# Gathering one turn's rows in a four-layer graph network: part of GpSimd's indirect gathers goes to SyncE as single-row copies

## What is computed

```
for layer in (gated, attention 4 heads, attention 8 heads + edge features + MLP, two GAT layers of 4 heads):
    per edge:  score from rows of the node tables at src[e] and dst[e]
    per edge:  weight = sigmoid(score)  or  softmax of the scores over the edges of one dst
    agg[node] = sum over the edges with dst == node of weight * row[src[e]]
    x = layernorm(x + dense(agg))
```

## Time and profile before

| | |
|---|---|
| runs, median of 3 | 7559.2 us (7523.48 to 7564.5) |
| profiled execution: its span | 6570.3 us, 37158 instructions recorded |
| profiled execution: its own time | not given |
| VectorE busy | 4654.6 us (71%) |
| GpSimd busy | 4293.2 us (65%) |
| ScalarE busy | 1375.2 us (21%) |
| TensorE busy | 1251.3 us (19%) |
| gathers in the four walks (L725) | 3136, 944 ns median |

### The profile page before, as it was taken

One profiled execution on the slowest core, in us unless ns is written; L12 is line 12 of the kernel. 1 busy time (PEld: TensorE's weight loads), 2 busy tenths in 40 slices (PEclk: granted clock), 3 DMA queues, 4 the chain that ended last, 5 costly groups with the idle time before them and its releaser, 6 DMA issues. The chain is left out here.

```text
span 6570.3 us, 37158 instructions
## 1 busy us (share of the span) xinstructions
PE 1251.3 (19%) x8049; PEld 1094.3 (17%) x8049; DVE 4654.6 (71%) x9455; ACT 1375.2 (21%) x3580; POOL 4293.2 (65%) x4445
## 2 busy tenths in 40 slices
PE   7100000145555534332000000810000010000000
PEld 6100000135544433322000000610000010000000
DVE  7788888799999969987888887744444444444445
ACT  0122222220111114431000000622222211222223
POOL 0777777667777760027777775367777767777775
PEclk9555555555555555556555555955555555555555
DMA  9666666433443437754666664123333323333332
GB/s 391 199 218 202 202 199 204 130 106 131 132 136 133 133 115 292 295 184 153 220 219 218 225 218 158 30 85 109 113 111 109 115 74 90 112 113 109 113 111 82
DMA packets 338944, 1032.97 MB, mean 157 GB/s; under 512 B 100325, under 2 KB 163137, under 8 KB 331294
## 3 DMA queue, kind: packets, MB, share of 16 engines
q0 software_dynamic: 166752, 401.68, 21.4%
q1 hardware_dynamic: 116642, 342.34, 14.8%
q10 hardware_dynamic: 55324, 286.57, 12.1%
HBM read 602.97 MB, written 427.39 MB: 157 GB/s over the span
## 5 line engine op out<-in xcount | busy, mean ns | idle before, releaser
L725 POOL DMA_INDIRECT rows<-table,idx x3136 | 2987.4, 953 | 985.0 <-issue 973.1
L644 POOL DMA_INDIRECT by_src<-ebuf,place x784 | 767.4, 979 | 275.0 <-issue 238.3
L1296 DVE SCALAR_TENSOR_TENSOR psA<-psA,cont,dstf 128x128 f32<-128x128 f32 (+1 forms) x2349 | 836.6, 356 | 48.0 <-ACT ebuf L1025 27.2
L1285 DVE TENSOR_TENSOR sc<-rows,ebuf 128x56 f32<-128x56 f32 x112 | 28.2, 252 | 1023.9 <-DMA rows<-table,idx 1023.9
L958 PE MATMUL psA<-dstf,ones 128*128 128x512 f32 x10 | 9.9, 1113 | 3055.3 <-DVE dstf L2223 3055.3
L1296 DVE SCALAR_TENSOR_TENSOR sums<-sums,cont,psA 128x128 f32<-128x128 f32 (+1 forms) x1512 | 518.9, 343 | 30.3 <-ACT psA L1221 29.0
L958 PEld LDWEIGHTS psA<-dstf,ones 128*128 128x128 f32 x10 | 2.7, 317 | 3056.9 <-issue 3056.9
L823 PE MATMUL psA<-attr,sums 128*128 128x49 f32 x1568 | 406.1, 403 | 470.8 <-DVE attr L1475 470.8
L2104 DVE TENSOR_TENSOR_SCAN psA<-rows,psA 128x1980 f32<-128x1980 f32 x112 | 480.0, 4286 | 3.9
L823 PEld LDWEIGHTS psA<-attr,sums 128*128 128x128 f32 x1568 | 397.0, 326 | 476.9 <-DVE attr L1475 476.9
L1227 ACT ACTIVATE psA<-df 128x60 f32<-128x60 f32 (+1 forms) x168 | 40.4, 241 | 1714.2 <-DVE df L1285 1714.2
(11 more groups left out here) (350 smaller groups left out, 5533.6 us busy)
## 6 DMA issues: line engine op xcount, KB each, us to landing
dstf<-spread_wide SPq DMA_DIRECT2D x168, 924.0 KB
states<-sums ACTq DMA_DIRECT2D x150, 952.0 KB, 4.0
rows<-by_src SPq DMA_DIRECT2D x55, 1035.0 KB, 5.1
states<-sums ACTq DMA_DIRECT2D x56, 1008.0 KB, 5.7
spread_wide<-sums SPq DMA_DIRECT2D x56, 924.0 KB, 24.7
states<-sums ACTq DMA_DIRECT2D x56, 903.0 KB, 7.4
rows<-table,idx POOLq DMA_INDIRECT x3136
msg<-low_rows SPq DMA_DIRECT2D x56, 448.0 KB, 3.7
```

The lines of the kernel that those rows point to most:

```text
L644: pool.indirect_dma_start(by_src[:, :], bass.IndirectOffsetOnAxis(ap=place[:, s, j:j + 1], axis=0), payload[:, s, j, :], None).then_inc(so ...
L725: pool.indirect_dma_start(rows[:, at:at + GW[ph]], None, table[ph][:, :], bass.IndirectOffsetOnAxis(ap=idx[:, s, j:j + 1], axis=0)).then_i ...
L1285: return dve.tensor_tensor(o_, a_, b_, op)
L1296: return dve.scalar_tensor_tensor(o_, a_, s_, b_, op0, op1)
```

## The change

Turn 54 (`SIDE`) of each walk no longer uses a half of `rows`. Its 14 columns go into a tile of its own (`ebuf`, `aux`, `msg`, `msg`). The first 10 (walks one and two) or 12 columns (three and four) are fetched by SyncE, partition by partition: one register load of 10 or 12 row numbers from `src`, then one single-row copy per number, whose HBM address comes from the register. That is 128 x 10 or 128 x 12 copies in a walk. GpSimd gathers the other 4 or 2 columns. The remaining 55 turns alternate between the two halves of `rows`, so turn 55 takes the half that turn 52 had.

In walks one and two SyncE's copies are divided over its iterations g = 1 to 52, each part behind the load L590 of that g and ahead of the load of the next; in walks three and four all stand in one piece behind L585.

GpSimd now takes the row numbers straight from `src`. The tile `idx`, ScalarE's copies into it and its semaphore are gone. In their place GpSimd waits once per walk for `src_in` and `n_kept`. `src` loses its 28 columns of padding, a one-hot tile of phase 0 moves from `ebuf` to `msg`, and one semaphore of the first-edge lookup is merged into another. VectorE waits at turn 54 for both `side_landed` and `side_gathered`.

```diff
+SIDE = 54
+SIDE_COLS = {0: 10, 2: 10, 3: 12, 4: 12}
...
-        src = sb("src", [P, CH + 2 * B], I32)
+        src = sb("src", [P, CH], I32)
...
-        hotSH = hot_turned(ebuf, 0, NB)
+        hotSH = hot_turned(msg, 1024, NB)
...
+        side_tile = {0: ebuf, 2: aux[:, :, :].rearrange("p b d -> p (b d)"), 3: msg, 4: msg}
...
+        def row_slot(ph, g):
+            return None if g == SIDE else (g - int(g > SIDE)) % 2
+        def slot_turns(ph, s, g=NG):
+            return sum(row_slot(ph, k) == s for k in range(g))
+        def landed_at(ph, g):
+            s = row_slot(ph, g)
+            before = sum(slot_turns(q, s) for q in TURN if q < ph)
+            return 16 * B * (before + slot_turns(ph, s, g) + 1)
+        def side_gathered_at(ph):
+            return 16 * sum(B - n for q, n in SIDE_COLS.items() if q <= ph)
+        def free_at(ph, g):
+            s = row_slot(ph, g)
+            users = [k for k in range(g) if row_slot(ph, k) == s]
+            return 2 + TURN[ph] * NG + (users[-1] + 1 if users else 0)
+        def turn_rows(ph, g):
+            s = row_slot(ph, g)
+            tile = side_tile[ph][:, 0:B * GW[ph]] if s is None else rows[:, s * B * GW[ph]:(s + 1) * B * GW[ph]]
+            return tile.rearrange("p (b w) -> p b w", b=B)
...
+            numbers_of = [sp.alloc_register(f"side_row{j}") for j in range(B)]
+            def side_open(ph):
+                sp.wait_ge(src_in, 48)
+                if ph == 0:
+                    sp.wait_ge(chains_ready, 1)
+                    sp.wait_ge(bias3_ready, 1)
+                    for k in range(2):
+                        sp.wait_ge(tab_first[k], 16 * -(-(KG - k) // 2))
+                else:
+                    sp.wait_ge(tab_saved, 16 * KG * TURN[ph])
+                    sp.wait_ge(n_kept, (2 if ph == 2 else 3) * KG)
+            def side_rows(ph, parts):
+                w, at, n = GW[ph], SIDE * B, SIDE_COLS[ph]
+                for p in parts:
+                    sp.load(numbers_of[0:n], src[p:p + 1, at:at + n])
+                    for j in range(n):
+                        node = sp.snap(numbers_of[j])
+                        sp.dma_start(side_tile[ph][p:p + 1, j * w:(j + 1) * w], table[ph][bass.ds(node, 1), :]).then_inc(side_landed[ph], 16)
...
                 if ZW[ph] == 4:
                     sp.dma_start(dflat[:, 0:CH * 4], view.rearrange("p c d -> p (c d)")).then_inc(slim_in, 16)
+                    side_open(ph)
+                    side_rows(ph, range(P))
 
...
                         if ph == 1 and g < NG - 1:
                             low_digits(g + 1)
+                        if ph in SIDE_COLS and g == 1:
+                            side_open(ph)
+                        if ph in SIDE_COLS and 1 <= g < SIDE - 1:
+                            side_rows(ph, range((g - 1) * P // (SIDE - 2), g * P // (SIDE - 2)))
                 if ph == 0:
...
-                    for it in range(IT):
-                        for s in range(2):
-                            g = it * 2 + s
-                            pool.wait_ge(idx_staged, g + (1 + TURN[ph] * (NG + 2)))
-                            pool.wait_ge(rows_used, g + (1 + TURN[ph] * NG))
-                            if g == 1 and ph < 3:
-                                spreads_landed()
-                            for j in range(B):
-                                at = (s * B + j) * GW[ph]
-                                pool.indirect_dma_start(rows[:, at:at + GW[ph]], None, table[ph][:, :],
-                                                        bass.IndirectOffsetOnAxis(ap=idx[:, s, j:j + 1], axis=0)).then_inc(rows_landed[s], 16)
+                    pool.wait_ge(src_in, 48)
+                    if ph:
+                        pool.wait_ge(n_kept, (2 if ph == 2 else 3) * KG)
+                    for g in range(NG):
+                        s = row_slot(ph, g)
+                        if s is None:
+                            for j in range(SIDE_COLS[ph], B):
+                                pool.indirect_dma_start(side_tile[ph][:, j * GW[ph]:(j + 1) * GW[ph]], None, table[ph][:, :],
+                                                        bass.IndirectOffsetOnAxis(ap=src[:, g * B + j:g * B + j + 1], axis=0)).then_inc(side_gathered, 16)
+                            continue
+                        pool.wait_ge(rows_used, free_at(ph, g))
+                        if g == 1 and ph < 3:
+                            spreads_landed()
+                        for j in range(B):
+                            at = (s * B + j) * GW[ph]
+                            pool.indirect_dma_start(rows[:, at:at + GW[ph]], None, table[ph][:, :],
+                                                    bass.IndirectOffsetOnAxis(ap=src[:, g * B + j:g * B + j + 1], axis=0)).then_inc(rows_landed[s], 16)
 
                     for s in range(2):
                         pool.wait_ge(sums_saved[s], 16 + 16 * IT * (TURN[ph] + 1))
...
-                else:
-                    act.wait_ge(rows_used, 2 + TURN[ph] * NG)
-                    for s in range(2):
-                        act.activation(idx[:, s, :], src[:, s * B:(s + 1) * B], ACT.Copy).then_inc(idx_staged, 1)
...
-                                at = (s * B + j) * GW[0] + D
-                                m = act.activation(gated[:, j * D:(j + 1) * D], rows[:, at:at + D], ACT.Copy, scale=wt[:, s, j:j + 1])
+                                m = act.activation(gated[:, j * D:(j + 1) * D], turn_rows(0, g)[:, j, D:2 * D], ACT.Copy, scale=wt[:, s, j:j + 1])
...
-                        act.wait_ge(rows_used, g + (3 + TURN[ph] * NG))
-                        act.activation(idx[:, s, :], src[:, bass.ds((g + 2) * B, B)], ACT.Copy).then_inc(idx_staged, 1)
...
-                        G3 = rows[:, s * B * GW[ph]:(s + 1) * B * GW[ph]].rearrange("p (b w) -> p b w", b=B)
+                        G3 = turn_rows(ph, g)
-                        dve.wait_ge(rows_landed[s], it * (16 * B) + (16 * B + TURN[ph] * IT * 16 * B))
+                        if row_slot(ph, g) is None:
+                            dve.wait_ge(side_landed[ph], 16 * P * SIDE_COLS[ph])
+                            dve.wait_ge(side_gathered, side_gathered_at(ph))
+                        else:
+                            dve.wait_ge(rows_landed[row_slot(ph, g)], landed_at(ph, g))
```

More of the change, by code:

```diff
@@ L125, in build @@
         attr = sb("attr", [P, 2, B * 32])
-        idx = sb("idx", [P, 2, B], I32)
         cg = sb("cg", [P, 2, B])
@@ L188, in build @@
         hotS = hot_turned(ebuf, numbers_at + ntile // 2, P)
-        hotSH = hot_turned(ebuf, 0, NB)
+        hotSH = hot_turned(msg, 1024, NB)
         early_hotS = [hotS, hot_turned(ebuf, 2240, P)]
-        early_hotSH = [hotSH, hot_turned(ebuf, 2240 + ntile // 2, NB)]
+        early_hotSH = [hot_turned(ebuf, 0, NB), hot_turned(ebuf, 2240 + ntile // 2, NB)]
         mark = ebuf[:, numbers_at + ntile // 2:numbers_at + ntile // 2 + CH]
@@ L352, in build @@
         ends1_saved = sem("ends1_saved")
-        first1_end = sem("first1_end")
         diag1_ready = sem("diag1_ready")
@@ L360, in build @@
         dve_step = sem("dve_step")
-        idx_staged = sem("idx_staged")
+        side_landed = {p: sem(f"side_landed{p}") for p in SIDE_COLS}
+        side_gathered = sem("side_gathered")
         rows_landed = [sem(f"rows_landed{s}") for s in range(2)]
@@ L705, in _ @@
                     pool.indirect_dma_start(firstk[:, 0:1], None, ends_src[:, :],
-                                            bass.IndirectOffsetOnAxis(ap=fixi[:, 2:3], axis=0)).then_inc(first1_end, 16)
+                                            bass.IndirectOffsetOnAxis(ap=fixi[:, 2:3], axis=0)).then_inc(first_end, 16)
                     pool.wait_ge(order_ready, 1)
@@ L1768, in sorted_pass @@
                     if g == 4:
-                        dve.wait_ge(first1_end, 16)
+                        dve.wait_ge(first_end, 32)
                         link(tt(chunkf[:, 1:2], firstk[:, 0:1], chunkf[:, 0:1], ALU.min))
```

## The result

The kernel after took 9256.58 us (median of 4 runs, 9217.84 to 9283.31) beside 7541.34 us for before (4 runs). The ratio is 1.229, with a 95% interval of 1.221 to 1.236. I had forecast 7520.8 us. **The change makes the kernel 1715 us slower.**

A forecast was written before the change was run, and what follows sets the result against it. GpSimd's gather issuing was taken to bound all four walks, VectorE close behind in the first two. Gains of 4.1 + 4.3 + 15.0 + 15.0 = 38.4 us, all else nothing, took 7559.2 to 7520.8 us; range 7495 to 7645.

The forecast's parts named there:

- The remainder: The 988.9 us between the profile's span (6570.3 us) and the runs' median (7559.2 us), which no row explained; treated as fixed.
- SyncE's copies: Single-row copies and register loads for turn 54: 6.8 us per partition, 871 us in walks three and four, hidden, cost 0.
- break-even: SyncE's time per partition in walks three and four at which the gain is gone: 7.64 us.
- Rival 1: SyncE finishes late for turn 54 and slows turns of walks one and two: 7643 to 7927 us; chance 0.18.
- Removed gathers: 44 fewer GpSimd gathers at turn 54: 4.1, 4.3, 15.0 and 15.0 us gained in the four walks, 38.4 us together.
- S55: VectorE's first operation of turn 55, forecast to come 15.0 us earlier in walks three and four.
- S53: VectorE's first operation of turn 53; from it to S55 forecast 34.2 us in walk one, 32.0 in walk two.
- Staging: Dropping 232 ScalarE index copies of 0.21 us each, forecast to gain nothing.
- Rival 2: Row copies delay gathers so that late landings come every fifth turn: 22 us, so 7543 us; chance 0.13.
- Rival 3: The unexplained 988.9 us grows with recorded instructions, 5868 more: +156 us, net 7677 us; chance 0.04.
- Rival 4: GpSimd stays idle at turn 54 because a side copy's landing is waited for elsewhere: no change; chance 0.02.
- The Trainium skill: Documentation warning on SyncE's register loads: at about 200 ns per register, walks three and four late, +187 us, 7746 us.

The follow-up runs named there:

- experiment 1: Kernel before, unchanged, profiled again in a series of the long kind: 0.998 of before, span 7545.9 us against its own time of 7547.66 us.
- short kind: Series of runs on one chip in which the unchanged kernel before has a median of 6571 to 6584 us; the change took 0.9936 of before there.
- long kind: Series of runs on one chip in which the unchanged kernel before has a median of 7503 to 7541 us; the change took 1.229 to 1.234 of before.
- experiment 2: Kernel after without SyncE's copies and index staging, GpSimd gathering all 14 columns of turn 54: 1.001 of before (0.998 to 1.004).

## Why the prediction was wrong, point by point

- *The remainder.* **The step that failed first:** "I carry the differences of the span over to the median and treat that remainder as fixed." The 988.9 us were no overhead around the span. They were the sign that the runs and the profile came from series of different kinds (experiment 1). The durations of the sum hold for the short kind, the time to be forecast is of the long.
- *SyncE's copies.* "Cost: 0 while it keeps pace" failed with it, and this is the term that holds the whole loss: it was put at nothing and measured 687 + 701 us of waiting at turn 54 and 178 + 159 us of longer turns in walks one and two. In the short series the estimate is good: a copy has a median pitch of 0.42 us (I took 0.50), the load 1.03 us (0.8), a partition with its occasional slow copy 6.56 us in the mean (6.8), and SyncE was done 840 us into walk three (871). In the long one a partition of walk three is 37 instructions x 1.40 = 52 us under gathers, seven times break-even.
- *Rival 1* named the place, the direction and its sign in the profile (VectorE waiting at turn 54, turns above 18 us in walks one and two), but its price, 7643 to 7927 us, fell short by 1330 us: I priced a copy by durations and never by its number of instructions, and bounded an instruction by rows of a short series. 0.18 was too little for a queue that gets 17,400 new instructions; the prediction counted 5868.
- *Removed gathers.* Right in the short series. In walk three S55 came 5281.25 - 4309.46 = 971.8 us after the first gather (4309.46), against 5312.76 - 4325.30 = 987.5 before: 15.7 us (15.0). In walk one S53 to S55 took 1227.77 - 1194.30 = 33.5 us (34.2), in walk two 4038.95 - 4007.05 = 31.9 us (32.0). With walk four that is 40.6 us (38.4), and 44 us were measured; the rest lies in walk one's earlier turns. Turn 55 waited 1.46 us for its rows, so VectorE is nearly what bounds it, as forecast.
- *Staging*: nothing, right (experiment 2).
- *Rival 2* did not come: the short series has no more turns over 20 us than before. *Rival 3* falls: the program grew by 16,926 recorded instructions and not by 5868, and in every profile since the time is the span and 2 us. *Rival 4* falls: in the short series turn 54 waited for nothing and 44 us were gained.
- *The Trainium skill* in the prediction: its roughly 200 ns per register ("Runtime: NRT & Kernel Launch", Instruction fetch mechanics) would make a load of 12 numbers 2.4 us, by an estimate from that page. The floor of about 600 ns stands in "DMA: Bandwidth & Descriptors" (Latency and other measured facts) of the Trainium skill. The trace of the short series shows 1.03 us, nearer to the floor. Its warning pointed the right way (SyncE late), but the lateness came from the pace of every instruction and not from the load.

## What to carry to other kernels

Before a sum is made, the profiled execution's time must be laid beside the runs; where they are 15% apart, as here, the durations are of another condition, and a spare queue's capacity has to be bounded by the worse one. Work that is put on an idle queue is to be counted in instructions, address arithmetic and moves included, not in copies or bytes: here 37 instructions for 12 rows of 544 bytes. A helper that is only just fast enough (871 of 963 us) is a gain of 0.6% against a risk of 23%.

## What the runs showed of the hardware

- The same program on one core takes 6571 to 6584 us in some series and 7503 to 7541 in others, at the same granted TensorE clock (0.50 of full speed in the walks of either kind, the level of 1.2 GHz).
- In the long kind, in walks three and four, SyncE gets through one instruction per 1.40 us while GpSimd gathers, after a first 100 to 150 within 40 us, in steps of 0.70 us, register operations included; 0.17 us per instruction once the gathers end. In walks one and two it is 0.34 us per instruction in the mean. GpSimd itself drops from 1.25 to 1.40 us per gather after some 200 gathers, and VectorE shows steps of 0.7 and 1.4 us. The DMA engines are not the limit: they are busy 0.35 of the time in walks three and four there, 0.38 in the short kind.
- A buffer that fills and a fixed rate behind it would look like this. One candidate is the path of the trace's own records: "NOTIFIC — the notification-queue block" of the Trainium skill (The write path) says that inside the block records are never dropped and the producer is held back in their place. Two things here fit it: the long kind's traces lack two thirds of the semaphore updates, so recording does fall behind there, and 1.40 us is twice 0.70, with two time stamps (start and end) for each instruction. But no run here can show it, since every timed run here was recorded too: the missing records can also be another effect of the same unknown cause. Instruction fetch looks too rare to be it: the page counts 295 instruction packets (8 KB each) for after and 163 for before, 132 more for 16,926 more instructions, which at 1.40 us is one packet in 180 us.
